# Two-layer cross attention on one core: heads in pairs of row halves, layer-1 normalisation folded into weights

## The reference

```python
# layer 0: 32 query heads of 16, 8 key/value heads (each serves 4 query heads)
q, k, v = x @ Wq + bq, ctx @ Wk + bk, ctx @ Wv + bv
attn = softmax(q k^T / sqrt(16) + mask)
x = layernorm(attn v @ Wo + bo + x) * gamma + beta
# layer 1: 16 heads of 32
a = layernorm(ctx) * ln_gamma + ln_beta
Q, K, V = x @ Wq.T, a @ Wk.T, a @ Wv.T
attn = softmax(where(mask, Q K^T * 32**-0.5, -inf))
out = x + tanh(gate) * ((attn V) @ Wo.T)
```

## Time and profile before

| | |
|---|---|
| Runs | 1501.32 us median of 3 (1498.83 to 1501.55) |
| Profiled execution | 1501.44 us |
| Its span, first to last instruction | 1499.6 us |
| PE matmul busy | 1412.2 us, 94% |
| PE weight loads busy | 995.1 us, 66% |
| DVE, ACT, POOL busy | 832.5, 827.6, 180.9 us |
| Mean granted TensorE clock | 0.945 |

### The profile page before, as it was taken

How to read it: one execution, slowest core, us unless ns; L and a number is a source line. 1 busy time by engine, 2 the same in 40 slices (tenths; PEclk the granted TensorE clock), 3 DMA queues, 4 the chain that set the end, 5 groups by cost and what they waited for, 6 DMA issues and landing times.

```text
span 1499.6 us, 32160 instructions
## 1 busy us (share of the span) xinstructions
PE 1412.2 (94%) x9840; PEld 995.1 (66%) x9840; DVE 832.5 (56%) x2470; ACT 827.6 (55%) x2504; POOL 180.9 (12%) x200
## 2 busy tenths in 40 slices
PE   3999999999999999999999999999999999999997
PEld 3667666676766667666676767667676676766665
DVE  4435646566464655656465564656646465565643
ACT  3435646466464755646475464646646475564644
POOL 2100111010111100111010011101011010011100
PEclk8569999999999999999999999999999999999996
DMA  8444254534435453244544525453443544424250
GB/s 241 144 98 85 67 118 101 134 72 113 105 76 119 109 124 78 81 108 94 134 88 111 102 66 119 109 134 68 105 107 86 119 108 107 96 67 119 53 131 6
DMA packets 77581, 153.76 MB, mean 103 GB/s; under 512 B 10272, under 2 KB 46944, under 8 KB 76784
## 3 DMA queue, kind: packets, MB, share of 16 engines
q1 hardware_dynamic: 77552, 153.40, 43.2%
HBM read 113.72 MB, written 39.65 MB: 102 GB/s over the span
## 4 chain that ended last, share of the span: by engine, by line
PE 82%; DVE 5%; issue 5%; ACT 4%; DMA 1%; POOL 1%; SPq 0%; ACTq 0%; DVEq 0%; POOLq 0%
PE TP L363 21%; PE PJ L317 12%; PE SCO L354 12%; PE OA L389 6%; PE PJ L554 4%; PE PJ L411 4%; PE PJ L419 4%; PE PJ L330 4%; PE OA L394 3%; PE SCO L358 3%; PE PJ L425 2%; ACT PR L866 1%; DMA PT<-wk 1%; DVE SCO L674 1%; ACT QHL L859 1%
## 5 line engine op out<-in xcount | busy, mean ns | idle before, releaser
L866 ACT ACTIVATE PR<-SCO,MN 100x361 f32<-100x361 f32 x768 | 433.4, 566 | 381.1 <-DVE MN L674 351.1
L674 DVE CUSTOM_DVE_ANT_0 SCO<-SCO,MK 100x361 f32<-100x361 f32 x768 | 413.1, 541 | 398.6 <-PE SCO L354 263.9
L363 PE MATMUL TP<-ident,PR 100*121 100x100 f32 x2304 | 435.1, 301 | 33.3 <-ACT PT L879 30.5
L363 PEld LDWEIGHTS TP<-ident,PR 100*121 100x121 f32 x2304 | 342.0, 199 | 134.7 <-issue 69.9
L879 ACT ACTIVATE PT<-TP 121x300 f32<-121x300 f32 x576 | 239.6, 416 | 5.3 <-PE TP L363 5.1
L354 PE MATMUL SCO<-K0S,Q0S 64*100 64x362 f32 x512 | 213.8, 418 | 11.5 <-DMA K0S<-k_scr 10.2
L354 PEld LDWEIGHTS SCO<-K0S,Q0S 64*100 64x100 f32 x512 | 84.0, 164 | 136.2 <-issue 107.1
L866 ACT ACTIVATION_READ_ACCUMULATOR PR<-SCO,MN 100x1 f32 x768 | 151.6, 197 | 0.0
L358 PE MATMUL SCO<-K1S,Q1S 128*100 128x362 f32 x256 | 111.1, 435 | 3.1 <-ACT Q1S L949 1.2
L1001 POOL TENSOR_TENSOR TL<-AT,TH 128x363 fp32r<-128x363 f32 x64 | 61.2, 957 | 401.0 <-ACT TH L924 401.0
L674 DVE DVE_READ_ACCUMULATOR2_ANT MN<- 100x1 f32 x768 | 108.5, 141 | 0.0
(11 more groups left out here) (124 smaller groups left out, 1837.6 us busy)
## 6 DMA issues: line engine op xcount, KB each, us to landing
K1S<-k_scr SPq DMA_DIRECT2D x128, 364.0 KB, 6.4
k_scr<-K1HL SPq DMA_DIRECT2D x64, 364.0 KB, 2.8
Q0S<-q_scr SPq DMA_DIRECT2D x128, 100.0 KB, 4.3
K0S<-k_scr SPq DMA_DIRECT2D x64, 182.0 KB, 5.2
AT<-ctx_cols SPq DMA_DIRECT2D x16, 722.0 KB, 6.5
NAT<-ctx_rows SPq DMA_DIRECT2D x16, 484.0 KB
q_scr<-QHL SPq DMA_DIRECT2D x16, 400.0 KB, 2.5
...
```

The source lines that it names most:

```text
L363: last = pe.transpose(TP[0:SP, k % 2, c * T:(c + 1) * T], PR[0:T, k % 3, c * SP:(c + 1) * SP], ident[0:T, 0:T])
L674: dve.tensor_tensor_reduce(out=bank, in0=bank, in1=mask[0:T, :], scale=scale, scalar=3.4e38, op0=ALU.add, op1=ALU.min, accum_out=MN[0:T, k ...
L866: act.activation(PR[0:T, k % 3, 0:S], SCO[0:T, k % 3, 0:S], ACT.Exp, bias=MN[0:T, k:k + 1], scale=-1.0, accum_out=SM[0:T, k:k + 1]).then_i ...
```

## The change

Heads are taken in pairs p = 0..23. In layer 0, `head0` gives the two heads of a pair to different row halves (heads 2p in rows 0 to 63, 2p+1 in rows 64 to 127), so the halves of `Q0S` and `K0S` are both read from pair 0 on. PE issues both scores of a pair, then other work, then the six transposes of pair p-2, which fill both `TP` banks; one copy of 600 elements per pair brings them to `PT`. `PR` has six buffers instead of three; `SCO` keeps three.

The layer-1 normalisation is folded away: gamma and the subtraction of the mean go into WK1 and WV1 once, at the start; beta's share becomes a column `KB` and a row `VB`. What is left per batch is the factor 1/deviation. For the keys, `rstd_rows` spreads it over the partitions by one matmul (`ONES` times a diagonal that POOL makes), DVE multiplies each chunk of keys with it (`keys1_scaled`), POOL adds `KB`, ACT and POOL split (`keys1_high`, `keys1_low`). For the values, ACT's copy has it as its scale, and POOL adds `VB`. `ctx_normalise`, `ctx_transposed` and the second splitting of the context go. `keys1` then can start in the pairs 22 and 23 of the entry before (`K1_EARLY`), and its chunks 0 to 2 all use bank `PJ[0]`. `NAT` shares the buffer of `V1`.

```diff
     HALF = 8
     NHALF = NH // HALF
     NJ = 4
-    ACT_OUTS, DVE_OUTS = 36, 12
+    NPAIR, L0P = NH // 2, 16
+    ACT_OUTS, DVE_OUTS = 18, 6
+    NPR = 6
...
@@ -161,20 +173,32 @@
                 at += counts[k]
             return ends
 
-        K1_STEPS = spans({7: 2, 8: 1, 9: 1, 10: 1, 13: 1, 14: 1, 15: 1, 16: 2, 17: 2, 18: 3, 19: 2, 20: 2, 21: 2,
-                          22: 3, 23: 3, 24: 3, 25: 3, 26: 3, 27: 2, 28: 2, 29: 2, 30: 3, 31: 3})
-        Q0_STEPS = spans({32: 4, 33: 3, 34: 6, 35: 3})
-        K0_STEPS = spans({34: 3, 35: 3, 36: 3, 37: 3})
-        V0_STEPS = spans({43: 3, 44: 3, 45: 3, 46: 3})
-
-        K1_DONE = [max(k for k, (i, _) in K1_STEPS.items() if i < 12 * (m + 1)) for m in range(C)]
+        K1_EARLY = spans({22: 3, 23: 4})
+        K1_AHEAD = K1_EARLY[23][1]
+        K1_LATE = spans({0: 3, 1: 2, 2: 2, 3: 1, 4: 1, 5: 4, 6: 2, 7: 2, 9: 2, 10: 3, 11: 2, 12: 3, 13: 4, 14: 4,
+                         15: 2, 16: 4})
+        K1_STEPS = {p: (i + K1_AHEAD, j + K1_AHEAD) for p, (i, j) in K1_LATE.items()}
+        Q0_STEPS = {16: (0, 6), 17: (6, 16)}
+        K0_STEPS = {16: (0, 6), 18: (6, 12)}
+        V0_STEPS = {20: (0, 6), 21: (6, 12)}
+        OUT1_STEPS = {6: (0, 2), 7: (2, 4), 8: (4, 6), 9: (6, 8)}
+        PV0_PARTS = {8: (0, 0, 2), 10: (0, 2, 3), 11: (1, 0, 2), 12: (1, 2, 3), 15: (2, 0, 2)}
+        PV1_TAIL = {0: (4, 2, 4), 1: (4, 4, 6), 3: (5, 0, 3), 4: (5, 3, 6)}
+
+        K1_BANK = (0, 0, 0, 1)
+        K1_SCALED = {2: 0, 8: 1, 14: 2}
+        K1_SPLIT = {3: 0, 9: 1, 15: 2}
         REP_BANK = (SCO[:, 2, 0:C * T], TP[:, 0, 0:C * T], TP[:, 1, 0:C * T], SCO[:, 0, 0:C * T])
...
+        def head0(k):
+
+            return k % 2, 2 * (k // 16) + k // 2 % 2, k // 8 % 2, k // 4 % 2
...
             sp.dma_start(V1_flat[:, C * P:2 * C * P], wv0.rearrange("p c n -> p (c n)")).then_inc(l_v0, 16)
+            sp.wait_ge(k0w_l, 1)
+            sp.wait_ge(v0w_l, 1)
             sp.wait_ge(nat_zero, 1)
...
-                sp.wait_ge(at_mm, 4 * b + 4)
-                load_ctx_rows(b + 1)
-                sp.wait_ge(at_h, 4 * b + 4)
-                sp.wait_ge(at_l, 4 * b + 4)
+                sp.wait_ge(ct_l, b + 1)
+                sp.wait_ge(ct_l2, 2 * b + 2)
                 load_ctx_cols(b + 1)
                 sp.wait_ge(mk1_a, b + 1)
                 sp.sem_inc(met_sp, 1)
                 sp.dma_start(MU[0:T, :], mask1[b + 1].partition_broadcast(T)).then_inc(l_mk1, 16)
+                wait_from(sp, pv, NHALF * b)
+                sp.wait_ge(c_st, 3 * b + 3)
+                load_ctx_rows(b + 1)
                 store_keys1(b, 0)
+                store_keys1(b, 1)
+                load_keys1(b, 0)
...
-            def transpose_probs(b, k):
-                pe.wait_ge(prob, NH * b + k + 1)
-                for c in range(SC):
-                    last = pe.transpose(TP[0:SP, k % 2, c * T:(c + 1) * T], PR[0:T, k % 3, c * SP:(c + 1) * SP],
-                                        ident[0:T, 0:T])
+            def transpose_probs(b, p):
+                pe.wait_ge(prob, NH * b + 2 * p + 2)
+                if p > 0:
+                    pe.wait_ge(*copied_out(b, p - 1))
+                elif not isinstance(b, int) or b > 0:
+                    pe.wait_ge(*copied_out(b - 1, NPAIR - 1))
+                for k in (2 * p, 2 * p + 1):
+                    for c in range(SC):
+                        last = pe.transpose(TP[0:SP, k % 2, c * T:(c + 1) * T], PR[0:T, k % NPR, c * SP:(c + 1) * SP],
...
-            def ctx_transposed(b, c):
-                for s in range(SC):
-                    last = pe.transpose(PJ[:, c % 2, s * SP:(s + 1) * SP], NAT[0:SP, s, c * P:(c + 1) * P],
-                                        ident[0:SP, 0:SP])
-                last.then_inc(at_mm, 1)
-
-            def keys1(b, i):
+            def rstd_rows(q):
+                pe.wait_ge(dg, q + 1)
+                pe.matmul(OA[:, 0:SC * SP], ONES[0:SP, :], DG[0:SP, :], start=True, stop=True).then_inc(rs_mm, 1)
...
             def batch(b, first, more):
 
-                for k in range(34):
-                    if k < 32:
-                        if k % 16 == 0:
-                            pe.wait_ge(kld[k // 16], 32 * b + 32)
-                            pe.wait_ge(qld[k // 16], 64 * b + 64)
+                for p in range(L0P):
+                    if p == 0:
+                        for G in range(2):
+                            pe.wait_ge(kld[G], 32 * b + 32)
+                            pe.wait_ge(qld[G], 64 * b + 64)
+                        pe.wait_ge(v0_ev, b + 1)
+                    for k in (2 * p, 2 * p + 1):
                         if k >= 3 or not first:
                             pe.wait_ge(prob, NH * b + k - 2)
                         score(b, k)
...
+                    if p in PV1_TAIL and not first:
+                        h, i, j = PV1_TAIL[p]
+                        out_half(b - 1, h, range(i, j))
+                        if p == 4:
                             sums_transposed(b - 1, 2)
...
+                    if p in PV0_PARTS:
+                        h, i, j = PV0_PARTS[p]
+                        out_half(b, h, range(i, j))
+                        if p == 12:
+                            sums_transposed(b, 0)
+                    keys1_steps(b, first, p)
...
+                        out1(b - 1, range(*OUT1_STEPS[p]))
+                    if p >= 2:
+                        transpose_probs(b, p - 2)
+                    elif not first:
+                        transpose_probs(b - 1, NPAIR - 2 + p)
+
+                out_half(b, 2, range(2, 3))
+                keys1_steps(b, first, 16)
+                transpose_probs(b, 14)
+                pe.wait_ge(k1_f, 4 * b + 3)
+                if first:
+                    pe.wait_ge(v1w_l, 1)
+                values1(b, range(2))
+                transpose_probs(b, 15)
                 values1(b, range(2, 3))
                 out_half(b, 3, range(3))
                 sums_transposed(b, 1)
                 values1(b, range(3, 4))
-                pe.wait_ge(k1_l, 4 * b + 4)
...
+                        if p == 20:
                             pe.wait_ge(q0_l, 4 * b + 8)
-                        values0(steps=range(*V0_STEPS[k]))
-                    if k >= 34:
-                        free_tp(b, k - 2)
-                        transpose_probs(b, k - 2)
-                    if k >= 44:
-                        out_half(b, 4, range(k - 44, k - 43))
-                    if more and k == 47:
-                        values0_transposed(b + 1)
+                        values0(steps=range(*V0_STEPS[p]))
+                    if more and p in K1_EARLY:
+                        if p == 22:
+                            pe.wait_ge(k0_l, b + 2)
+                            values0_transposed(b + 1, PJ[:, 1, :])
+                        for i in range(*K1_EARLY[p]):
+                            keys1(b + 1, i)
+                    if p >= 18:
+                        transpose_probs(b, p - 2)
 
...
-            def ctx_normalise(q, s):
-                dve.wait_ge(c_rs, q + 1)
-                dve.tensor_scalar(NAT[0:SP, s, :], NAT[0:SP, s, :], CMV[0:SP, s, 0:1], CRS[0:SP, s:s + 1],
-                                  ALU.subtract, ALU.mult).then_inc(c_nrm, 1)
+            def keys1_scaled(b, m):
+                dve.wait_ge(k1_mm, 4 * b + m + 1)
+                if m >= 1 or not isinstance(b, int) or b > 0:
+                    dve.wait_ge(k1_l, 4 * b + m)
+                if m == 0:
+                    dve.wait_ge(rs_ev, b + 1)
+                dve.tensor_tensor(K1F[:, :], PJ[:, K1_BANK[m], 0:SW], RSB[:, :], ALU.mult).then_inc(k1_f, 1)
 
...
                 dve.wait_ge(l_mk0, 16 * b + 16)
-                for k in range(35):
-                    if k < 32:
+                for p in range(L0P):
+                    if p % 4 == 0 and (p > 0 or not first):
+                        if p > 0:
+                            probs_out(b, p - 3)
+                        else:
+                            probs_out(b - 1, NPAIR - 3)
+                    if p in K1_SCALED:
+                        keys1_scaled(b, K1_SCALED[p])
+                    for k in (2 * p, 2 * p + 1):
                         shift(b, k)
-                    if k == 0 and not first:
...
             def exps(b, k):
                 act.wait_ge(shifted, NH * b + k + 1)
-                if k >= 3 or not isinstance(b, int) or b > 0:
-                    act.wait_ge(pt_mm, NH * b + k - 2)
-                act.activation(PR[0:T, k % 3, 0:S], SCO[0:T, k % 3, 0:S], ACT.Exp, bias=MN[0:T, k:k + 1],
+                wait_from(act, pt_mm, NPAIR * b + k // 2 - 2)
+                act.activation(PR[0:T, k % NPR, 0:S], SCO[0:T, k % 3, 0:S], ACT.Exp, bias=MN[0:T, k:k + 1],
                                scale=-1.0, accum_out=SM[0:T, k:k + 1]).then_inc(prob, 1)
 
...
+            def keys1_high(b, m, first):
+                act.wait_ge(k1_b, 4 * b + m + 1)
+                if m >= 2:
```

(38 more changed lines are left out.)

423 lines of the change are left out of this document (222 added, 201 removed).

## The result

Four runs of the changed kernel took 1575.66, 1587.59, 1599.88 and 1601.42 us (median 1593.74), against 1501.41 for the kernel before. The ratio is 1.054 (95% interval 1.048 to 1.060). It is slower, where I had forecast faster. The spread says something too: the runs of before lie within 3 us of each other, these within 26, and the longer ones have the lower mean clock (0.857, 0.850, 0.841, 0.841). The profiled execution is the fastest one, 1575.66 us with a span of 1573.9.

What follows compares the result with a forecast made beforehand. TensorE's path, busy for 94% of the span, was taken as the bound. 1501.4 - 102 (fifteen batches at -6.8) + 60 (clock falls) - 15 (start and first batch) = 1444 us, range 1375 to 1525.

Steps and rivals of the forecast that it cites:

- The slot: Layer 0: pairing two heads' scores saves 0.55 us a pair, 0.38 for one row switch and 0.17 for overlap.
- The overlap's 0.17: Layer 0: a pair's second score runs beside the first, gaining 0.17 us a pair (between 0 and 0.2).
- The wait for both halves: Start of layer 0: TensorE stands about 3.5 us (2 to 4.5) for both halves of the spread operands.
- Layer 1 with it: Layer-1 stage including TensorE's wait for the spread operands: 23.0 us instead of 22.3, so +0.7 a batch.
- out0's wait: Middle: with V1 chunk 0 first on ACT, out0 starts 1.3 to 1.6 us later, taken as 1.5.
- Layer 0 at full clock: Layer-0 stage with the clock at 1.00: 35.5 us, 11.2 less than the 46.7 before.
- The rise about pair 6: Layer 0: a fallen clock comes back about pair 6, after about 21 us at half clock.
- So I expect a fall in ten of fifteen batches: Layer 0: the wait at its start lowers the clock in ten batches, 6 us each, +60 us.
- POOL's new additions cost nothing: Middle and other key/value work: POOL's added additions cost 0 us, since POOL is busy for 12% of the span.
- delay the first score by about 7 us: Kernel start: folding gamma, column means and the later WK1 load delay it 7 us; start and first batch together -15.
- the upper bound of 1480: Top of the forecast's own bounds, 1414 to 1480 us, for falls in 5 to 15 batches, overlap or not.
- Rival 2: Layer 0: a fallen clock stays low until the middle, 17 us more a fall; 1554 (ten falls) or 1640 (fifteen); chance 0.14.

Runs made afterwards that it cites:

- experiment 7: Kernel of experiment 4 with ACT's copy of the sums moved ahead of its copy of V1 chunk 0 in the middle; 1380.7 us (0.920).
- experiment 1: Changed kernel with 22 matmuls, results never read, ahead of pair 0's scores in entries 1 to 15; 1457.2 us (0.971).
- experiment 4: Changed kernel with the spread's loads cut by head instead of by row half, heads 0 to 15 first; 1401.4 us (0.932).
- experiment 6: Kernel of experiment 4 with POOL's additions of VB to V1 chunks 0 and 1 moved behind the context's deviations; 1344.3 us (0.894).
- experiment 9: Changed kernel with only POOL's additions of VB to V1 chunks 0 and 1 moved behind the context's deviations; 1531.4 us (1.018).
- experiment 11: Changed kernel with the edits of experiments 4, 6 and 7, plus 8 unread matmuls before entry 0's first score; 1315.0 us (0.877), against 1316.0 without the matmuls.
- experiment 2: Kernel before the change, with head 0 made to wait for both row halves; 2085.3 us (1.389).
- experiment 8: Kernel before the change, with 56 unread matmuls while TensorE stands ahead of its very first score; 1498.6 us (0.998).
- experiment 5: Kernel of experiment 4 with each layer-0 pair's second score moved behind the pair's other work, ahead of its transposes; 1748.5 us (1.166).

## Why the prediction was wrong

**Right.** The slot: 0.55 us a pair forecast, 0.53 measured in pair 10, 0.48 on the mean of pairs 9 to 14. (The overlap's 0.17 was too high by the prediction's own numbers, since a score is 0.15 us; it is 0.09.) The wait for both halves: 3.5 forecast (2 to 4.5), 3.9 measured, and it is there in every entry. Layer 1 with it: 23.0 forecast, 23.03 measured. out0's wait from 0.3 to 1.6 through ACT's order: 1.5 forecast, 1.3 measured, and taken back by experiment 7. Layer 0 at full clock is 37.34 us (experiment 1); against the forecast's 35.5 it holds the four key steps (0.7), the part of `out_half` (0.5) and the transposes (0.6) that I had counted in the middle, so its size was right within half a microsecond. The whole entry as well: two entries of experiment 1 have no fall anywhere and take 84.2 us; less the 2.1 us of the slow DVE step that is 82.1, against the forecast's 89.2 - 6.8 = 82.4. The rise about pair 6: in the entry shown the clock is back at 824.5, in pair 6; over the 15 entries it comes back 12 to 30 us behind the first score, and the low time in layer 0 is 21.1 us on the mean, as forecast.

**Wrong, the clock: "So I expect a fall in ten of fifteen batches", "then cost 6 us: +60".** This is the step that turned the sign. Its mechanism was right, a stand that lowers the clock and denser slots that bring it back; the number of falls and the price of one were both too small. The clock fell in 15 of 15. Of the 15, the shortest and the longest layer 0, first to last score (us, busy PE, PEclk, DMA, GB/s), are

```profile
239.36:277.11 37.75, 37.75 (x306) 0.85 0.34 88
988.99:1034.79 45.80, 45.80 (x306) 0.67 0.30 79
```

At full clock it takes 33.3 (experiment 4), the mean of the 15 is 41.8: 8.5 us lost in each, for 21.1 us low, so 0.40 us per microsecond at 1.2 GHz. The rows give the same (at a mean clock of 0.67 the low share is 0.66 of the time, at 0.85 it is 0.30): 45.80 x 0.66 = 30 us low cost 12.5, and 37.75 x 0.30 = 11 us low cost 4.5. My 6 us for 21 was 0.29. The prediction doesn't say where the 6 comes from; even the ratio of the first entry would have given 21 x (1 - 46.7 / 69.0) = 6.8, and that entry has a thinner list. One more fall that I didn't foresee comes in the middle: 3.4 us at low clock, about 1.5 lost (in experiment 1, entries with one take 85.4 to 86.2 us, those without 84.2). In ten of the 15 entries of the changed kernel it follows the stand for `Y`, in the other five the stand of 1.6 us ahead of out0. 15 x (8.5 + 1.5) = 150 instead of 60: 90 us.

**Wrong, the middle: "POOL's new additions cost nothing".** I asked which engines wait for POOL and found none; I did not ask what runs beside it. The term was put at nothing from POOL's 12% load. The runs show 2.1 us an entry, 32 us (experiments 6 and 9).

**Wrong, the start: "delay the first score by about 7 us".** It came 17.5 us later (51.41 against 33.90); the folding's matmuls on PE stand from 29.82 to 48.55, 18.7 us, where I had counted a few. The first entry then took 23.5 us less than before (89.6 against 113.1 from its first score to the next entry's), so start and first entry gained 6 us, not 15: 9 us. Some of that is luck: the first layer 0 of this execution was the shortest of the three with the same instructions (experiment 11).

1444 + 90 + 32 + 9 = 1575, with every term rounded; the profiled execution took 1575.7. That is an account of this one execution, the fastest of four. Two more numbers of the prediction don't follow from its own terms: the upper bound of 1480 leaves out what it names, since fifteen falls without overlap are 1444 + 30 + 44 = 1518; and 0.3 + 1.2 + 0.9 + 0.6 us for a pair at the low clock are 3.0, not 2.9 (3.24 measured). Rival 2 with fifteen falls had the count and the sign right; its price was too high for this kernel (17 us a fall against 8.5), because the clock does come back here. It got 0.14, with the denser slots against it, and those did bring the clock back; what neither it nor the forecast had was a fall in every entry that lasts 21 us and costs 8.5. An edit of two lines to the kernel before would have shown beforehand that the stand lowers the clock in every entry (experiment 2); it cost 585 us there.

**Still open.** What exactly in a slot makes the clock fall, hold or rise. Single scores with three transposes let it fall (experiment 8), and it came back while paired scores with four key steps or two and two steps of out1 ran; what lies between was not measured. Whether the fall in experiment 5 needs its wait of 0.7 us is open, and how much of its 347 us is clock is worked out, not measured apart. Why the four executions of the changed kernel differ by 26 us is known only as far as their mean clocks go.
